# A recurrent state-space layer with a gated feed-forward block on one core: ScalarE's products reach y through accumulating transfers instead of GpSimd's additions

## What is computed

```python
def step(state, xs):
    d_t, B_t, C_t, u_t = xs
    dA = jnp.exp(d_t[..., None] * A)
    state = dA * state + (d_t * u_t)[..., None] * B_t[:, None, :]
    y_t = jnp.einsum('bdn,bn->bd', state, C_t)
    return (state, y_t)
...
y = jnp.swapaxes(ys, 0, 1) + u * D_param
y = y * jax.nn.silu(gate)
return y @ W_out.T
```

## Time and profile before

| | |
|---|---|
| median of 2 runs | 1180.28 us (1178.9 to 1181.65) |
| profiled execution | 1188.98 us, its span 1186.9 us |
| mean granted TensorE clock in it | 0.961 |

### The profile page before, as it was taken

The page is one execution under the profiler, slowest core; times in us unless marked ns, Lnnn a source line. Parts: engine busy times, 40 slices in busy tenths (PEclk is TensorE's granted clock), DMA queues, the critical chain, the costliest instruction groups (busy, mean ns, idle before and its releaser), DMA issues.

```text
span 1186.9 us, 16724 instructions
## 1 busy us (share of the span) xinstructions
PE 1070.9 (90%) x5072; PEld 766.5 (65%) x5072; DVE 1026.3 (86%) x1217; ACT 711.3 (60%) x1155; POOL 1016.0 (86%) x586
## 2 busy tenths in 40 slices
PE   5979987889999999998997999998998999999767
PEld 4747766666757776675855787576756777555444
DVE  3469788899789999899986999899998999888895
ACT  4657646776475756477583565576576575565440
POOL 3679999999878899889987789879998889889961
PEclk9979999799799999999998999999999999999878
DMA  3627654443223543343322364324333443334310
GB/s 126 214 94 242 215 169 159 147 146 133 63 90 140 190 164 141 132 151 134 99 90 101 133 215 163 131 98 157 118 100 105 162 155 130 109 114 169 124 62 36
DMA packets 46570, 160.86 MB, mean 136 GB/s; under 512 B 5355, under 2 KB 5611, under 8 KB 37004
## 3 DMA queue, kind: packets, MB, share of 16 engines
q1 hardware_dynamic: 45424, 159.14, 38.7%
q10 hardware_dynamic: 1052, 0.59, 0.2%
HBM read 135.33 MB, written 24.38 MB: 135 GB/s over the span
## 4 chain that ended last, share of the span: by engine, by line
PE 49%; DVE 17%; POOL 16%; issue 13%; ACT 3%; DVEq 1%; DMA 1%; SPq 0%; POOLq 0%; ACTq 0%
PE pj L1079 16%; PE hT L1364 10%; DVE sb_h L1018 8%; POOL sb_dBu L794 8%; PE pj L1277 7%; PE pj L1311 5%; DVE sb_yT L947 4%; PE pj L1342 3%; POOL sb_yT L764 3%; PE pj L1084 2%; PE pj L1382 2%; DVE sb_un L872 2%; PE pj L1097 2%; POOL sb_w_sp L733 1%; POOL sb_un L738 1%
## 5 line engine op out<-in xcount | busy, mean ns | idle before, releaser
L1018 DVE TENSOR_TENSOR_SCAN sb_h<-dA,sb_dBu 128x512 f32<-128x512 f32 x512 | 596.8, 1207 | 43.7 <-POOL sb_dBu L794 30.2
L794 POOL TENSOR_TENSOR sb_dBu<-sb_v,sb_bb 128x1024 f32<-128x1024 f32 x256 | 607.1, 2384 | 28.6 <-DVE sb_h L1018 22.8
L584 ACT ACTIVATE dA<-sb_delta,sb_apar 128x512 f32<-128x512 f32 x512 | 344.9, 688 | 232.4 <-DVE sb_h L1018 226.4
L1079 PE MATMUL pj<-sb_x_hi,sb_w_sp 128*128 128x512 f32 x1208 | 345.8, 410 | 25.4 <-DVE sb_un L872 12.3
L1364 PE MATMUL hT<-sb_ident,sb_h 128*128 128x128 f32 x2048 | 288.7, 283 | 66.8 <-DVE sb_yT L947 51.7
L1364 PEld LDWEIGHTS hT<-sb_ident,sb_h 128*128 128x128 f32 x2048 | 244.4, 145 | 149.9 <-issue 50.9
L1079 PEld LDWEIGHTS pj<-sb_x_hi,sb_w_sp 128*128 128x128 f32 x1208 | 221.2, 193 | 89.0 <-issue 24.6
L947 DVE SCALAR_TENSOR_TENSOR sb_yT<-hT,sb_cs,sb_yT 128x512 f32<-128x512 f32 x321 | 229.2, 735 | 53.8 <-PE hT L1364 53.2
L764 POOL TENSOR_TENSOR sb_yT<-sb_yT,sb_part 128x512 f32<-128x512 f32 x155 | 199.4, 1286 | 63.5 <-ACT sb_part L677 63.4
L677 ACT ACTIVATE sb_part<-hT,sb_cs_act 128x512 f32<-128x512 f32 x155 | 106.1, 685 | 161.4 <-PE hT L1364 152.9
L1079 PE MATMUL pj<-sb_x_lo,sb_w_sp 128*128 128x512 f32 x604 | 167.4, 400 | 0.0
(11 more groups left out here) (126 smaller groups left out, 810.1 us busy)
## 6 DMA issues: line engine op xcount, KB each, us to landing
sb_w_sp<-w_cache SPq DMA_DIRECT2D x55, 1024.0 KB, 4.8
sb_ring<-w_ring SPq DMA_DIRECT2D x67, 512.0 KB, 3.3
sb_bb<-b_rows SPq DMA_DIRECT2D x128, 256.0 KB, 3.6
w_cache<-sb_w_sp SPq DMA_DIRECT2D x19, 1024.0 KB, 4.9
sb_xio<-x SPq DMA_DIRECT2D x7, 1024.0 KB, 6.9
out<-sb_xio SPq DMA_DIRECT2D x3, 1024.0 KB, 5.6
sb_xio<-x SPq DMA_DIRECT2D x4, 256.0 KB, 3.6
out<-sb_xio SPq DMA_DIRECT2D x4, 256.0 KB, 2.0
```

What stands on the lines that cost most here:

```text
L584: nc.scalar.activation(dA[g % 2][:, :], delta[:, j, :], ACT.Exp, scale=apar[:, j, n:n + 1]).then_inc(dA_done, 1)
L794: nc.gpsimd.tensor_tensor(dBu[:, dbu_buffer(s), :, :], v[:, j:j + 2, :], bb[:, i % B_RING, :].unsqueeze(1).to_broadcast([P, 2, T]), ALU.mu ...
L1018: nc.vector.tensor_tensor_scan(h[:, i % 2, 2 * part + e, :], dA[g % 2][:, :], dBu[:, dbu_buffer(s), e, :], 0.0, ALU.mult, ALU.add).then_in ...
L1079: done = nc.tensor.matmul(bank[:, :], w[:, kk * P:(kk + 1) * P], xs[:, kk, :], start=(p == 0), stop=(p == len(products) - 1))
```

## The change

POOL's `tensor_tensor` that added `part` to `yT` becomes a transfer that POOL issues, from `part` to `yT` (128 rows of 2 KB, 256 KB), with accumulation: what arrives is added to what stands in `yT`. An instruction that does nothing stands ahead of it and carries the waits. The transfers' semaphore counts by 16, and there are two of them, one for even and one for odd q, since two transfers may be under way at a time. `added` gives semaphore and count for all who waited for `yp_done`. The memory for transfer descriptors grows from 256 to 512.

```diff
-        yp_done = sem("yp_done")
+        yp_done = [sem(f"yp_done{r}") for r in range(2)]
...
+        def added(c_b, q, r=None):
+
+            r = (q - 1) % 2 if r is None else r
+            return yp_done[r], c_b * 16 * len(range(r, len(OFF_ADDS), 2)) + 16 * len(range(r, q, 2))
...
-                            act.wait_ge(yp_done, c_b * len(OFF_ADDS) + q - 1)
+                            act.wait_ge(*added(c_b, q, q % 2))
...
                 elif before:
-                    pool.wait_ge(yp_done, c_b * len(OFF_ADDS) + before[-1] + 1)
+                    pool.wait_ge(*added(c_b, before[-1] + 1))
                 y = yT[:, c, hf * JH * P:(hf + 1) * JH * P]
-                nc.gpsimd.tensor_tensor(y, y, part[:, q % 2, :], ALU.add).then_inc(yp_done, 1)
+                nc.gpsimd.nop(nofuse=True)
+                nc.gpsimd.dma_start(y, part[:, q % 2, :], accum_op=ALU.add).then_inc(yp_done[q % 2], 16)
...
-                            dve.wait_ge(yp_done, c_b * len(OFF_ADDS) + done_by(OFF_ADDS, i - 1, c))
+                            dve.wait_ge(*added(c_b, done_by(OFF_ADDS, i - 1, c)))
...
-                            pe.wait_ge(yp_done, b * len(OFF_ADDS))
+                            for r in range(2):
+                                pe.wait_ge(*added(b - 1, len(OFF_ADDS), r))
...
-    nc = bacc.Bacc("TRN2", target_bir_lowering=False, num_devices=1, dynamic_dma_scratch_size=256)
+    nc = bacc.Bacc("TRN2", target_bir_lowering=False, num_devices=1, dynamic_dma_scratch_size=512)
```

More of the change, by code:

```diff
@@ L1034, in _ @@
                 else:
-                    dve.wait_ge(yp_done, (b + 1) * len(OFF_ADDS) - len(handed_over(i)) - len(handed_over(i - 1)) + done_by([(i - 1, d) for d in handed_over(i - 1)], i - 1, c))
+                    dve.wait_ge(*added(b, done_by(OFF_ADDS, i - 1, c)))
                 y = yT[:, c, JH * P:D]
@@ L1202, in misc @@
                             pe.wait_ge(y_done, b * len(ON) + done_by(ON, N - 1, TC))
-                            pe.wait_ge(yp_done, b * len(OFF_ADDS) + done_by(OFF_ADDS, N - 1, TC))
+                            for r in range(2):
+                                pe.wait_ge(*added(b, done_by(OFF_ADDS, N - 1, TC), r))
                             if first:
```

## The result

The changed kernel takes 1220.97 us in the median of 2 runs (1215.08 to 1226.86) against 1180.28 before: ratio 1.0338, 95% interval 1.0293 to 1.0382. It is 3.4% slower, where 1% was forecast. The profiled execution took 1226.86 us, its span is 1224.7. Ratios leave out executions over 1.5% above the fastest of the same kernel, which concerns only two of the four of run e10.

What follows compares the result with a forecast made beforehand. No engine bounds the kernel throughout; POOL does in some stretches, most in the first batch. Terms 5.4 + 1.6 + 1.8 + 3.4 = 12.2 us on the profiled 1188.98 gave 1201.2, scaled 1192 us, 1% slower; range 1166 to 1243.

Steps and rivals of the forecast that it cites:

- POOL's saturated stretches and their counts: Where POOL has no idle time: 27 additions in the first batch, 4 each in the second and third, 9 in the fourth.
- The issue, 1.5 us: POOL's time to issue one transfer, 0.2 us more than the addition; costs 5.4, 1.6 and 1.8 us in saturated stretches.
- Two transfers are then under way at a time: Densest stretch: additions start 3.59 us apart, the same piece returns after 7.2 us, so landings of 4.8 us fit and overlap.
- This is paid once, not in each slot: First batch: ACT's 3.4 us delay does not build up, since POOL may run three slots ahead of DVE and goes on issuing.
- rival A: Slower, 1203 to 1313 us: a transfer holds POOL clearly longer than the addition, from about 1.7 us per issue; chance 0.38.
- second mechanism: Dense stretches: only one transfer allowed at a time would hold POOL for the rest of the landing, 1.2 us.
- 4.8 us: Time from a transfer's issue to its landing, taken from a range of 3.2 to 4.8 us.
- ACT's wait, 8.0 to 15 or 25 us: ACT's wait for additions to free part buffers should rise from 8.0 us to some 15 to 25, in the first batch.
- the 3.4 us: First batch: with landings of 4.8 us, ACT, then dA, then DVE fall 3.4 us further behind POOL.
- The transfer engines, nothing: The added 41 MB of transfers cost nothing; they could only delay a later row of B, for which POOL's dBu waits.
- PE's wait for a half's last addition: At the end of a half, 7.36 us before PE transposes yT cover the landing, so PE should not wait.
- Rival B: Faster: issue as cheap as SP's, 0.52 us, saving 18 us, scaled 1162 us; chance 0.12.

Runs made afterwards that it cites:

- e10: The changed kernel, descriptor memory 512, with three part buffers instead of two and table Wx left out: ratio 1.0329 against the kernel before.
- e1: The changed kernel with descriptor memory 1024 instead of 512, nothing else: 1188.18 us, ratio 1.0055 against the kernel before.
- e9: The changed kernel with descriptor memory 576 in place of 512: 1195.29 us, ratio 1.0101 against the kernel before.
- e5: The changed kernel with descriptor memory 1024, three part buffers and semaphores instead of two, table Wx left out: 1175.65 us, ratio 0.9946 against the kernel before.
- e6: The changed kernel with descriptor memory 1024, two part buffers, table Wx left out: 1191.22 us, ratio 1.0069 against the kernel before.
- e4: The kernel before with POOL's additions cut to 4 elements per row, the rest left out: 1170.83 us, ratio 0.9896.
- e12: The kernel before, POOL adding as before, with three part buffers and table Wx left out: 1183.94 us, ratio 1.0019.
- e3: The changed kernel with transfers adding only 128 of 512 elements of each row: 1188.62 us, ratio 1.0046 against the kernel before.

## Why the prediction was wrong, step by step

- **POOL's saturated stretches and their counts** were right, and so was the place: the first batch pays most.
- **The issue, 1.5 us.** It is 1.06. The term of +0.2 us per addition has the wrong sign; by my sum -0.22 would have gained a few microseconds (28 x 0.22 less 3.4). The Trainium skill's 1 us to the first byte for transfers issued from GpSimd ("DMA: Bandwidth & Descriptors", latency and other measured facts), which I set aside, was the nearer price (the row has 0.90 us for the issue), though it is a latency and not the engine's time. What I made of it, 12 us less, does not follow from my own terms: the 8.8 us of loss go and 28 x 0.29 = 8.1 us of gain come, 17 us in all.
- **The step that failed: "Two transfers are then under way at a time", and with it "This is paid once, not in each slot".** Only one is under way with a memory of 512. I had this as rival A's second mechanism, priced it at 1.2 us per issue and gave A 0.38. POOL stood 87.0 us, in 54 places, 1.6 us in each on average. A came true with its time (1203 to 1313) and by this mechanism, not by its first one, a dear issue. Two things made it dearer. A transfer issued late lands late, and the `part` buffer that ACT waits for with it; while POOL stands in front of its issue, the `dBu` products behind it stand too, so the lead of three slots on which I had counted shrinks. That the lead is used up shows only in e10's pattern; in the change itself DVE waits for `dA` instead. And landing is not 4.8 us each time: the median of 4.2 is 0.6 under my figure, but 31 of 155 took over 6 us, up to 9.9. In the first batch seven in succession (121.4 to 180.6 us) took 6.8 to 9.4 us, with SP's store of 1 MB and load of 512 KB started within 1.6 us of them. Over the whole trace a transfer of SP of 512 KB or more starts within 1.5 us of 25 of the 31 long ones, and of 23 of the other 124. Room for two transfers takes 33 us away (e1), of which 26 come with an eighth more memory (e9).
- **ACT's wait, 8.0 to 15 or 25 us.** It became 100.9. With two transfers allowed it is still 45.7, and the third buffer takes 15.6 us off the time (e5 against e6). Slots of 3.6 us in the first batch and long landings made the 3.4 us recur. How much of a long landing is SP's traffic was not tried by taking that traffic away.
- **TensorE's clock, no term.** My sum has every wait at its own length. In the changed kernel PE had a lower granted clock (0.942 and 0.952 in the two executions, 0.961 in the profiled one before) and was busy 16.8 us longer for the same instructions. What part of that is time of the kernel is open.
- **DVE** waited 15.5 us in 4 places where it takes over a piece, which I had left out of the sum; with room for two transfers it is 1.9 us (e1).
- **The transfer engines, nothing.** Right for the rows of B: POOL waits 6.5 us for them, 4.9 before. PE's wait for a half's last addition does not show among the waits, as forecast.
- **Rival B, 18 us of gain at 0.52 us per issue.** Too high: even 0.20 us of POOL per addition gains only 12 (e4).

In one order the account closes: 8.3 us of relief (e12 to e5), then 15.6 lost through two buffers (e5 to e6), 33 through the memory (the change against e1): 40 us, and 41 were measured. The three were measured in kernels of different data and chips, so the agreement is good to a few microseconds only. The shares are not prices that each cause has by itself. In the other order the third buffer brings nothing while the memory is 512 (1.0329 in e10, 1.0338 in the change), and with three buffers the memory is worth 3.8%, some 45 us (e10 against e5, by the ratios); with a quarter of the bytes one transfer at a time costs next to nothing (e3). Each cause bites through the others.

## What to carry to other kernels

When work is handed from an engine to transfers, the price of the issue is the small part. Ask how many transfers may be under way and what bounds that number (here the memory for descriptors: with 512 two copies were under way at a time, but never two transfers that add); what stands behind the issuing engine while it waits for room; and whether each buffer that a transfer reads can stay occupied for the longest landing, not the median. Look also at TensorE's granted clock: where it is at its lower level and TensorE is the bound, the stretch takes longer, and a table by stretches puts that down to the change. Before all that, cut the removed work to nothing in the old kernel: that run would have shown that 1% was all there was to gain.

## What was not expected of the hardware

- A wait for descriptor room stands in no semaphore and not in the issue's own duration (half of them take 848 to 897 ns): it shows as idle time ahead of it, put down to "issue", ending in 60 of 154 cases 0.27 to 0.36 us after the landing of the transfer before.
- Transfers that add kept the 16 engines busy twice as long as copies of the same bytes (19.1% against 9.4%), and landed after 4.2 us instead of 3.1.
- POOL's product directly behind an accumulating issue is shown 0.3 us longer (2.69 against 2.38 us), behind a copy's it is not.
